# A fused graph layer and slice-attention kernel: 35 row gathers a pair instead of 36, two waits for landed rows, softmax steps in halves, and filler matmuls in the tail

## What is computed

```python
h0  = layernorm(x)
agg = segment_sum(h0[src], dst, N)                       # the gather
h   = relu(agg @ W_rel + b_rel + h0 @ W_root)
i, f, g, o = split(h @ W_ih.T + b_ih + b_hh, 4)
y   = sigmoid(o) * tanh(sigmoid(i) * tanh(g))
x   = x + y @ W_fc + b_fc
z   = layernorm(x)
sw  = softmax(((z @ W_x + b_x) @ W_slice + b_slice) / temp)   # slice weights, per head
tok = (sw.T @ (z @ W_fx + b_fx)) / sum(sw)               # one token a slice
out = attention over the 64 tokens of each head (W_q, W_k, W_v)
x   = x + (sw @ out) @ W_out + b_out
```

## Time and profile before

| | |
|---|---|
| median of 3 runs | 1493.12 us (1491.98 to 1493.93) |
| the profiled execution's own time | 1490.67 us |
| its span, first to last instruction | 1488.7 us |
| GpSimd busy | 975.0 us, 65% |
| TensorE matmuls busy | 1225.3 us, 82% |
| VectorE, ScalarE busy | 820.7 us, 584.7 us |
| granted TensorE clock, mean | 0.94 |

### The profile page before, as it was taken

The page is one execution under the profiler, slowest core; times in us unless marked ns, Lnnn a source line. Parts: engine busy times, 40 slices in busy tenths (PEclk is TensorE's granted clock), DMA queues, the critical chain, the costliest instruction groups (busy, mean ns, idle before and its releaser), DMA issues.

```text
span 1488.7 us, 25194 instructions
## 1 busy us (share of the span) xinstructions
PE 1225.3 (82%) x8343; PEld 1075.8 (72%) x8343; DVE 820.7 (55%) x2125; ACT 584.7 (39%) x1120; POOL 975.0 (65%) x975
## 2 busy tenths in 40 slices
PE   0226898889988898889888998989888988894796
PEld 0214787878877787778777887878777877783596
DVE  3852364656455655566555655565556645554464
ACT  3631344434443444344443444344434434352131
POOL 1247777777777777777777777777777777500043
PEclk9997999999999999999999999999999999996698
DMA  5764444444444344444444444434444444203396
GB/s 150 230 202 131 113 122 130 124 125 119 134 118 132 111 135 125 127 122 121 135 118 126 118 134 120 133 110 134 125 125 120 124 134 131 88 29 98 96 344 206
DMA packets 109102, 198.03 MB, mean 133 GB/s; under 512 B 39587, under 2 KB 66079, under 8 KB 109052
## 3 DMA queue, kind: packets, MB, share of 16 engines
q0 software_dynamic: 46160, 124.60, 29.1%
q1 hardware_dynamic: 59312, 60.26, 13.8%
q10 hardware_dynamic: 3600, 12.80, 2.1%
HBM read 165.56 MB, written 32.87 MB: 133 GB/s over the span
## 4 chain that ended last, share of the span: by engine, by line
POOL 41%; issue 30%; DMA 13%; PE 10%; DVE 3%; SPq 1%; ACT 1%; POOLq 0%; DVEq 0%; ACTq 0%
POOL ring L545 41%; DMA ring<-table,sidx 10%; PE ps L296 3%; PE ps L298 2%; PE ps L297 2%; DMA table<-ring 1%; DMA ring<-dstp 0%; SPq L337 0%; ACT ring L613 0%; PE ps L933 0%; DVE stats L1074 0%; DMA ring<-in_b_fx 0%; DMA ring<-in_x 0%; PE ps L921 0%; DMA dstp<-didx 0%
## 5 line engine op out<-in xcount | busy, mean ns | idle before, releaser
L545 POOL DMA_INDIRECT ring<-table,sidx x900 | 928.1, 1031 | 292.6 <-issue 276.9
L296 PE MATMUL ps<-h_h,wih_h 128*128 128x256 f32 x1200 | 346.7, 289 | 0.5 <-DVE h_l L1265 0.5
L297 PE MATMUL ps<-h_l,wih_h 128*128 128x256 f32 x1200 | 339.7, 283 | 0.0
L298 PE MATMUL ps<-h_h,wih_l 128*128 128x256 f32 x1200 | 339.5, 283 | 0.0
L849 PE MATMUL ps<-ring,oneh 128*125 128x512 f16 x900 | 235.2, 399 | 108.3 <-DMA ring<-table,sidx 108.2
L849 PEld LDWEIGHTS ps<-ring,oneh 128*125 128x125 f16 x900 | 120.7, 141 | 183.5 <-DMA ring<-table,sidx 132.9
L296 PEld LDWEIGHTS ps<-h_h,wih_h 128*128 128x128 f32 x1200 | 230.1, 192 | 4.2 <-issue 1.1
L297 PEld LDWEIGHTS ps<-h_l,wih_h 128*128 128x128 f32 x1200 | 230.3, 192 | 1.8
L298 PEld LDWEIGHTS ps<-h_h,wih_l 128*128 128x128 f32 x1200 | 230.2, 192 | 0.0
L679 ACT ACTIVATE gate<-ps,bgate 128x256 f32<-128x256 f32 x300 | 125.1, 468 | 189.4 <-PE ps L298 189.4
L1182 DVE TENSOR_SCALAR oneh<-iota,rel 128x125 f16<-128x125 f16 x900 | 153.3, 285 | 4.8 <-issue 3.0
(11 more groups left out here) (208 smaller groups left out, 2626.3 us busy)
## 6 DMA issues: line engine op xcount, KB each, us to landing
ring<-table,sidx POOLq DMA_INDIRECT x900, 2.8
swt_d<-swt ACTq DMA_DIRECT2D x25, 500.0 KB
gate<-swt_d SPq DMA_DIRECT2D x19, 500.0 KB, 7.1
ring<-in_x SPq DMA_DIRECT2D x12, 512.0 KB, 5.4
table<-ring SPq DMA_DIRECT2D x12, 512.0 KB, 5.4
xn<-table SPq DMA_DIRECT2D x25, 224.0 KB
xin<-in_x SPq DMA_DIRECT2D x25, 224.0 KB
res<-xin SPq DMA_DIRECT2D x25, 224.0 KB
```

The lines of the kernel that those rows point to most:

```text
L296: eng.matmul(dst, wh, xh, start=first, stop=False)
L297: eng.matmul(dst, wh, xl, start=False, stop=False)
L298: return eng.matmul(dst, wl, xh, start=False, stop=last)
L545: pool.indirect_dma_start(ring[:, e, j, :], None, table, bass.IndirectOffsetOnAxis(ap=sidx[:, e, j:j + 1], axis=0)).then_inc(done, 16)
```

## The change

Slots are shared: block 0 has 15 slots of its own, the next 3 hold the edges around the border between both windows and are multiplied with two one-hot matrices (one for each window), block 1 has 17 of its own. That is 35 gathers and 38 sum matmuls a pair. The flag for the general path (many passes over all edges) is now raised if an even window has more than 2304 or fewer than 1920 edges, or a pair more than 4480. Ahead of the first gather of each block GpSimd waits for the last group of the block before. The subtraction, exponential, scaling and low part of the softmax are issued once for each window. The bias `b_fc` is added to x early in `add_bfc`, `b_out` goes into the value rows of head 0, and `norm_x2` has two VectorE instructions fewer. In the last turns and the attention, `spin` issues matmuls whose result nobody reads, ahead of waits.

```diff
+    PAUSES = ((0, 0), (1, 0))
+    LISTS = (64, 48)
+    MIX = 3
+    OWN0 = CH - MIX
+    OWN1 = 17
+    SLOTS = OWN0 + MIX + OWN1
+    HOT1 = MIX + OWN1
...
             def load_edges(base, e, done):
+                if e == 0:
+                    for t, to in ((srcp, sidx[:, 0, :]), (dstp, didx[:, 0:CH])):
+                        load_list(to[:, 0:OWN0], t, base, OWN0, done)
+                        load_list(to[:, OWN0:CH], t, base + LOW0, MIX, done)
+                else:
+                    load_list(sidx[:, 1, 0:OWN1], srcp, base + CAP, OWN1, done)
+                    load_list(didx[:, CH:CH + MIX], dstp, base + LOW0, MIX, done)
+                    load_list(didx[:, CH + MIX:CH + HOT1], dstp, base + CAP, OWN1, done)
...
                         for q in range(3):
+                            if e == 0 and k == 1 and q == 2:
+                                after(pool, half_used[1], p)
                             older = 6 * e + 3 * k + q - 2
...
+                            if q == 0 and (e, k) in PAUSES:
+                                if e or k:
+                                    pool.wait_ge(rows_in[(2 * e + k - 1) // 2][(k + 1) % 2][2], LAND * p + LAND)
+                                else:
+                                    after(pool, rows_in[1][1][2], landed(1, 1, 2) * p)
                             pool.sem_inc(gather_go, 1)
-                            for j in LANDS[q]:
-                                gather(e, k * HALF + j, rows_in[e][k][q])
+                            for j in in_group(e, k, q):
+                                gather(e, j, rows_in[e][k][q])
...
+                if e and k == 0:
+                    for m in range(MIX):
+                        pe.matmul(ps[0:WN, SUM_B, :], oneh[:, CH + m, 0:WN], ring[:, OWN0 + m, :],
+                                  start=(m == 0), stop=False)
...
+            def spin(bank, n):
+
+                for _ in range(n):
+                    pe.matmul(ps[:, bank, 0:2 * P], w1_h[:, 0, 0:P], at_h[:, 0, :], start=True, stop=True,
+                              skip_group_check=True)
...
                 if ffn:
+                    if not gnn:
+                        spin(SUM_A, 30)
                     transpose_x2(t - 2)
...
+                    if not gnn:
+                        spin(SUM_A, 11)
                     logits(t - 2)
...
+                    if not gnn:
+                        spin(SUM_A, 56)
                     token_sums(t - 2)
...
-                dve.tensor_tensor(x2[0:WN, :, :], y, xin[0:WN, :, :], ALU.add).then_inc(x2_step, 1)
...
-                dve.tensor_tensor(xin[0:WN, :, :], x2[0:WN, :, :], bout[0:WN, :].unsqueeze(1).to_broadcast([WN, 2, C]),
-                                  ALU.add).then_inc(res_done, 1)
+                dve.tensor_tensor(xin[0:WN, :, :], y, xin[0:WN, :, :], ALU.add).then_inc(x2_step, 1)
...
-                dve.tensor_tensor(heads(sw), heads(sw), mx8[0:WN, :].unsqueeze(2).to_broadcast([WN, 2 * H, G]),
-                                  ALU.subtract).then_inc(lg_sub, 1)
+                for e in range(2):
+                    dve.tensor_tensor(half(sw, e), half(sw, e), of_heads(mx8, e), ALU.subtract).then_inc(lg_sub, 1)
```

More of the change, by code:

```diff
@@ L278, in build_program, with in_group, landed @@
         PARTS = ((0, 112), (112, WN))
+        def in_group(e, k, q):
+            return [k * HALF + j for j in LANDS[q] if e == 0 or k * HALF + j < OWN1]
+        def landed(e, k, q):
+            return 16 * len(in_group(e, k, q))
         def turns(turn):
@@ L844, in sums_of @@
                     pe.wait_ge(hot_done[e], p + 1)
+                if e and k == 0:
+                    for m in range(MIX):
+                        pe.matmul(ps[0:WN, SUM_B, :], oneh[:, CH + m, 0:WN], ring[:, OWN0 + m, :],
+                                  start=(m == 0), stop=False)
                 for q in range(3):
[L846 to L850, removed]
+                    pe.wait_ge(rows_in[e][k][q], landed(e, k, q) * p + landed(e, k, q))
+                    for j in in_group(e, k, q):
+                        hot = CH + MIX + j if e else j
+                        last = pe.matmul(ps[0:WN, SUM_A + e, :], oneh[:, hot, 0:WN], ring[:, e * CH + j, :],
+                                         start=(hot == 0), stop=(hot in (CH - 1, CH + HOT1 - 1)))
                 last.then_inc(half_used[e] if k == 0 else sum_done[e], 1)
@@ L922, in token_sums @@
                     last.then_inc(swt_mm, 1)
+                if isinstance(p, int) and p == NP - 1:
+                    spin(SUM_A, 10)
                 pe.wait_ge(x2_hi, p + 1)
@@ L1029, in _ @@
                 u, j = (h % 2) * G, h // 2
-                last = pe.matmul(ps[u:u + G, 3 + j // 2, (j % 2) * C:(j % 2) * C + C], ost[:, h * G:(h + 1) * G],
-                                 wout[:, h, :], start=True, stop=True, skip_group_check=True)
+                dst = ps[u:u + G, 3 + j // 2, (j % 2) * C:(j % 2) * C + C]
+                last = pe.matmul(dst, ost[:, h * G:(h + 1) * G], wout[:, h, :], start=True, stop=(h > 0),
+                                 skip_group_check=True)
+                if h == 0:
+                    pe.matmul(dst, ident[0:G, 0:G], bout[0:G, :], start=False, stop=True, skip_group_check=True)
             last.then_inc(att_pe, 1)
+            spin(TOK + 1, 16)
             pe.wait_ge(att_a, 3)
@@ L1175, in _, with one_hots @@
             general = dve.value_load(flag_i[0:1, 0:1], min_val=0, max_val=1)
-            def one_hots(e, idx, base, rel_sem, rel_n, hot_sem):
-                dve.tensor_scalar(rel[:, e, :], didx[:, idx, :], base, None, ALU.subtract).then_inc(rel_sem, 1)
+            def one_hots(first, n, idx, base, rel_sem, rel_n, hot_sem):
+                dve.tensor_scalar(rel[:, first:first + n], didx[:, idx:idx + n], base, None, ALU.subtract).then_inc(rel_sem, 1)
                 dve.wait_ge(rel_sem, rel_n)
-                for j in range(CH):
-                    last = dve.tensor_scalar(oneh[:, e, j, 0:WN], iota[:, 0:WN], rel[:, e, j:j + 1], None, ALU.is_equal)
+                for j in range(first, first + n):
+                    last = dve.tensor_scalar(oneh[:, j, 0:WN], iota[:, 0:WN], rel[:, j:j + 1], None, ALU.is_equal)
                 last.then_inc(hot_sem, 1)
@@ L1274, in heads, with half, of_heads @@
                 return x[0:WN, :, :].rearrange("p e (h g) -> p (e h) g", g=G)
+            def half(x, e):
+                return x[0:WN, e, :].rearrange("p (h g) -> p h g", g=G)
+            def of_heads(x, e):
+                return x[0:WN, e * H:(e + 1) * H].unsqueeze(2).to_broadcast([WN, H, G])
             def softmax(p):
@@ L1293, in softmax_end @@
                 dve.wait_ge(sm_step, 4 * p + 4)
-                dve.tensor_tensor(heads(sw), heads(sw), rs8[0:WN, :].unsqueeze(2).to_broadcast([WN, 2 * H, G]),
-                                  ALU.mult).then_inc(sw_done, 1)
+                for e in range(2):
+                    last = dve.tensor_tensor(half(sw, e), half(sw, e), of_heads(rs8, e), ALU.mult)
+                last.then_inc(sw_done, 1)
                 dve.wait_ge(sw_done, p + 1)
@@ L1303, in low_sw @@
                 after(dve, tok_mm, p)
-                dve.tensor_tensor(sw_l[0:WN, :, :], sw[0:WN, :, :], sw_h[0:WN, :, :].bitcast(F32),
-                                  ALU.subtract).then_inc(sw_lo, 1)
+                for e in range(2):
+                    last = dve.tensor_tensor(sw_l[0:WN, e, :], sw[0:WN, e, :], sw_h[0:WN, e, :].bitcast(F32), ALU.subtract)
+                last.then_inc(sw_lo, 1)
             def cell_c(p, f):
@@ L1359, in turn @@
                     cell_o(t - 1, 3)
+                if gnn:
+                    add_bfc(t - 1)
                 if gather:
```

119 lines of the change are left out of this document (74 added, 45 removed).

## The result

| | before | changed |
|---|---|---|
| median of 4 runs each | 1493.53 us (1491.98 to 1495.96) | **1536.95 us** (1533.83 to 1539.1) |
| ratio, 95% interval | | 1.0288 (1.0265 to 1.031): slower by 43 us |
| the profiled execution's own time, its span | 1490.67, 1488.7 | 1537.25, 1535.5 |
| granted TensorE clock (1.00 is full speed), mean | 0.94 | 0.965 |

The account below looks back on a forecast made before the run. GpSimd's gathers were taken to set the pace. The terms -31 - 34 + 114 + 1 - 14 = +36 on 1490.67 gave 1527 us for a profiled execution and 1529 for the median, range 1502 to 1558.

Parts of the forecast that it names:

- One gather fewer: GpSimd's loop: one gather less in each of 25 pairs, at 1.25 us, saves 31 us.
- The cover that was named: TensorE in the loop: has room for two more sum matmuls a pair, at most 0.4 us each.
- Halves: VectorE's softmax in the loop: shorter instructions stretch gathers less, saving 34 us, with ends 43 and 10.
- all short instructions at 0.1 us a pair each: VectorE in the loop: nine short two-input SBUF instructions cost gathers 0.9 us a pair, fourteen after the change 1.4.
- The two waits: GpSimd, ahead of each block's first gather: 49 waits paid in full at 2.32 us add 114 us.
- The rival of the cheap wait (1476): GpSimd's waits in the loop: each costs only 1.25 us, 61 for 49, giving 1476 us; chance 0.10.
- The landing that the forecast was worked out from: Gather transfers in the loop: a gather lands 2.8 us after its start (median; 2.6 to 4.9).
- Everything else in the loop: GpSimd's other groups' waits for the group two before: stay hidden, adding nothing.
- a sign of a wrong mechanism: GpSimd's timeline: idle before gathers other than a block's first would show the mechanism wrong.
- The 1.4 us of cover: GpSimd after a pause at T: seventh gather could start at T+6.1, its turn is T+7.5, so its wait stays hidden.
- TensorE is hit too: TensorE in the loop: longer waits drop its clock, it sets the pace, 38 us more, 1567; chance 0.10.
- The tail: After the last gather: filler keeps TensorE's clock at 1.00, two VectorE steps leave the chain, saving 14 us, ends 17 and 8.

Follow-up runs that it names:

- e10: Changed kernel without its two waits a pair, nothing else altered: 1416.03 us, ratio 0.9502 to the kernel before.
- e7: Kernel before with four waits a pair (one ahead of each half of each block), nothing else of the change: 1698.30 us, ratio 1.1395.
- e8: Changed kernel with four waits a pair and the three softmax instructions whole again: 1676.33 us, beside 1491.24 for the kernel before.
- e5: Changed kernel as it is, with its two waits a pair: 1854.32 us, beside 1842.68 for the kernel before.
- e6: Changed kernel without its two waits a pair: 1858.64 us, beside 1842.68 for the kernel before.
- e1: Changed kernel without its two waits a pair: 1852.85 us, beside 1843.32 for the kernel before.
- e3: Changed kernel with four waits a pair instead of two: 1655.77 us, beside 1843.32 for the kernel before.
- e9: Changed kernel with four waits a pair and no filler matmuls: 1668.85 us, beside 1491.24 for the kernel before.

## Why the prediction was right, and where it was off

The sign, the size and the mechanism held: 36 us forecast for a profiled execution, 46.8 found (43 by the medians).

1. *One gather fewer.* 25 x 1.25 as forecast; the loop with no waits (e10) takes 1133.4 us for 875 gathers, which is 874 x 1.25 = 1092.5, 38.5 of stretch and 2.9 of other gaps. The cover that was named, TensorE having room, held down to 45.3 us a pair.

2. *Halves.* The total was right (38 against 34), **the reason for it only in part**. Each stretched gather can be given to the VectorE instruction that ended about 0.82 us before it. The three whole instructions stretched gathers by 49.9 us and the six halves by 20.5, so 29.4 lie there. L1241 and L1247, the two instructions that were taken out, had stretched them by another 10.0. The remaining ones give about 1 us more than before. The prediction had put all short instructions at 0.1 us a pair each, which made of the two some 5 us. But whether the 29.4 are the shorter length is not shown: e7 took 33 us off the stretch with waits alone and the whole instructions kept (theirs fell from 49.9 to 27.0), and with four waits the halves are worth 11.5 or 20.9. The changed kernel's own two waits are out as the reason, since e10 has the same stretch without them. What is left beside the length is the phase that 35 gathers a pair instead of 36 brought, and no run that came out tells the two apart.

At the halves the distance is the one of the whole instructions (0.81 to 0.82 us): the gather at 690.70 ended at 692.11, 0.83 us after the second half of L1394, which had ended at 691.28:

```profile
689.99 1.29 DVE L1394 TENSOR_TENSOR sw_l<-sw,sw_h 125x512 fp32r<-125x512 f32 x2 [0.89 <-ACT sw_h L763]
```

It started when the first half was over: a half costs what is left of it, not nothing. Of the 68 gathers that met a half, 51 ended 0.82 us behind the second and 17 behind the first, so gathers do get in between. In e10 it is 1 and 45, with the same instructions: that is the phase. The kernel before has the control for the two inputs. L1280 is as long as L1285 (1.23 us) but reads one input from PSUM:

```profile
693.58 1.23 DVE L1280 TENSOR_TENSOR sw<-ps,biasx 125x1024 f32<-125x1024 f32 x1 [1.91 <-PE ps L298]
```

```profile
693.67 0.95 POOL L545 DMA_INDIRECT ring<-table,sidx  x1 [0.30 <-DMA ring<-table,sidx]
```

None of the 23 gathers that began while L1280 ran took over 0.95 us; the 23 that began while L1285 ran took 1.94 on average. L1283 and L1290, 1.22 us long with one input, which is in SBUF, had 23 gathers each begin in them, and none took over 0.96. VectorE was not held up in turn: L1285 took 1.225 to 1.227 us each time.

3. *The two waits.* 49 at 2.32 forecast, 24 at 2.28 and 25 at 2.43 measured, and e10 proves that they are paid in full: without them 121 us are gone. The rival of the cheap wait (1476) is out by this alone. The landing that the forecast was worked out from held: a median of 2.8 us (2.7 to 3.2) in the changed kernel.

4. *Everything else in the loop* had been put at nothing: 7 us more of idle in gathers other than the first of a block, which the prediction had named as a sign of a wrong mechanism. About half is the other groups' wait for the group two before. The 1.4 us of cover that were worked out for the seventh gather (it could start at T+6.1, its turn is T+7.5) were missed in seven pairs behind the first, 2.2 us together, and the tenth gather was late once, by 1.1. The other half are the six gaps of 0.48 us shown under e10, 2.9 together. They stand at gathers that wait for nothing, every seventh pair (pairs 5, 12, 19 and 10, 17, 24, counted from 0), and not in the kernel without waits; their cause is open.

5. *TensorE is hit too* (1567) did not happen. It waits 36 us longer for gathers, but the loop's clock is 0.98, and it kept up. That is 5.8 us a pair instead of 4.3; the prediction had looked for 8 or more.

6. *The tail* brought 7 us, not 14: **the term was mis-sized**. Counted from the last gather, the last attention took 23.5 us instead of 28.9, 5.4 less where 9.3 had been expected; its clock is 0.93 and not 1.00. That small matmuls shrink less than the clock grows is in the traces: the first eight of 64x64 took 1.06 us before at 0.50 and 0.63 in the changed kernel at 1.00. The 32 matmuls of the attention gained little (3.44 us, 3.68 before), and in e8 they took 2.08 behind the same filler, so the 1.4 us that are missing here depend on something that the prediction did not have and no run settles. At four places the filler ended after its wait was over, about 1 us in all. And the final stage, whose first 5.00 us were to shrink by 2, took 88.9 instead of 86.7 us, inside the spread that the runs show for it. Those first matmuls did get faster, 42 in the first 5.00 us at 1.00 instead of 27 at 0.61, but the stage did not end sooner: it is not paced by them alone. Up to the start of the final stage the gain is 9 us; 5.4 of it, in the attention, is the filler's, and the rest is the filler's, the two lost VectorE steps' and the spread of that stretch.

## What to carry to other kernels

A wait for its own transfer cost GpSimd, which set the pace here, 2.3 to 2.5 us each with a landing of 2.8 us; put one nowhere in such a stream unless something is measured to need it. Where one engine's instruction holds up another's, as VectorE's did gathers here, the cost can move with their phase (33 us in e7, with waits alone), so an edit that shifts one of them may bring or take as much as the shortening of the instruction: test the shift alone before crediting the instruction. Before an idle time is called the cause of a lower clock, look in the other runs for the same idle time with the clock kept (here e8: 2.60 us idle, then 1.00). Measure the kernel before beside every run; here the same program took 1416 or 1853 us, and the ranking of the variants turned over with it.

## What was not expected of the hardware

The same kernels took 1416, 1491 and 1537 us in one condition, and 1853, 1843 and 1854 in another. It belongs to no chip: the chip of e5 and e6 was that of e7 to e10. In the second one TensorE stands idle ahead of its matmuls: e1 has 82.3 + 72.6 + 72.2 = 227 us of "issue" in front of L312 to L314. With four waits a pair (e3) the same lines have less:

```profile
PE ps L314 <- issue: 32.8, 55, 1.2
...
PE ps L312 <- issue: 25.8, 46, 1.6
```

and the kernel is 10% *faster* than the kernel before beside it, where in the other condition four waits made it 12 to 14% slower (e8, e9, and e7). A slower stream of gathers is not the explanation. From 499 to 749 us GpSimd issued 159 gathers in e3 and 140 in e1, all transfers together moved 107 and 92 GB/s, and e10, in the other condition, issued 193 at 131 GB/s with next to no such gaps. Why four waits take most of them away, and what makes them at all, stays open. Two waits a pair, the change itself, brought nothing there (1854 against 1853 for e1).
